# Read products of a piece on eight array tiles, and pieces that alternate between the halves of the heads

## What is computed

```python
# q, k, v: 16 heads of 32; q and k normalized; a = sigmoid(x@Wa+ba), b = sigmoid(x@Wb+bb)
def step(state, inp):                       # state: (batch, head, 32, 32)
    q_t, k_t, v_t, a_t, b_t = inp
    pred = einsum('bhde,bhd->bhe', state, k_t)
    update = einsum('bhe,bhd->bhde', b_t[..., None] * (v_t - pred), k_t)
    state = a_t[..., None, None] * state + update
    out = einsum('bhde,bhd->bhe', state, q_t)
    return (state, out)
# y = rmsnorm(out) * g_norm * silu(x @ Wg); result y @ Wo, added to x
```

## Time and profile before

| | us |
|---|---|
| median of 3 runs | 2973.11 |
| lowest, highest | 2969.35, 2973.77 |
| span of the profiled execution | 2958.8 |
| profiled execution as timed: span and what lies around it (median less span: 14.3) | about 2973 |
| PE busy in the span | 2700.6 (91%) |
| DVE busy in the span | 1882.3 (64%) |

### The profile page before, as it was taken

How to read it: one execution, slowest core, us unless ns; L and a number is a source line. 1 busy time by engine, 2 the same in 40 slices (tenths; PEclk the granted TensorE clock), 3 DMA queues, 4 the chain that set the end, 5 groups by cost and what they waited for, 6 DMA issues and landing times. The chain is left out here.

```text
span 2958.8 us, 117088 instructions
## 1 busy us (share of the span) xinstructions
PE 2700.6 (91%) x51052; PEld 1927.0 (65%) x51052; DVE 1882.3 (64%) x5306; ACT 1059.9 (36%) x1964; POOL 1328.6 (45%) x1767
## 2 busy tenths in 40 slices
PE   7999889899999999999999999999999999999867
PEld 5887556566666666666666666666666666666653
DVE  6777456566666666666666666666666666665626
ACT  5777223333333333333333333333333333333220
POOL 2222444445545444444554545555554444455410
PEclk9999999999999999999999999999999999999988
DMA  7352112211122222212222222212222222122178
GB/s 234 94 162 65 42 49 61 59 49 46 56 60 61 61 61 61 60 56 54 58 58 58 60 61 59 57 49 54 58 58 61 61 61 61 54 55 60 46 250 309
DMA packets 365965, 224.78 MB, mean 76 GB/s; under 512 B 277584, under 2 KB 294032, under 8 KB 365456
## 3 DMA queue, kind: packets, MB, share of 16 engines
q1 hardware_dynamic: 356240, 200.51, 24.0%
q10 hardware_dynamic: 9216, 16.78, 1.5%
HBM read 125.49 MB, written 74.97 MB: 68 GB/s over the span
## 5 line engine op out<-in xcount | busy, mean ns | idle before, releaser
L899 PE MATMUL psum<-w_all,xnT 128*128 128x512 f32 (+2 forms) x2048 | 732.6, 501 | 41.5 <-DVE xh L3297 33.9
L2602 POOL TENSOR_TENSOR sm<-sm,half 128x1 f32<-128x1 f32 (+1 forms) x384 | 535.3, 1394 | 85.1 <-ACT sm L2149 69.1
L899 PEld LDWEIGHTS psum<-w_all,xnT 128*128 128x128 f32 x2048 | 372.2, 190 | 285.7 <-issue 235.5
L3269 DVE TENSOR_TENSOR blk<-blk 128x30 f32<-128x30 f32 (+14 forms) x960 | 382.3, 398 | 33.0
L3267 DVE TENSOR_TENSOR blk<-blk 128x30 f32<-128x30 f32 (+14 forms) x960 | 369.8, 385 | 40.0 <-issue 14.2
L954 PE MATMUL psum<-xnT,w_all 128*128 128x128 f32 x2048 | 264.4, 281 | 0.9 <-DVE xc L3168 0.9
L1069 PE MATMUL psum<-pk,uw 32*32 32x64 f32 x8192 | 221.6, 216 | 44.3 <-issue 44.2
L1101 PE MATMUL psum<-w_out,gate 128*128 128x512 f32 x512 | 253.0, 613 | 5.4 <-DVE gate L3291 3.6
L954 PEld LDWEIGHTS psum<-xnT,w_all 128*128 128x128 f32 x2048 | 245.4, 193 | 16.6 <-issue 6.3
L1060 PE MATMUL psum<-pk,uw 32*32 32x64 f32 x8192 | 226.4, 221 | 24.9 <-issue 23.0
L1060 PEld LDWEIGHTS psum<-pk,uw 32*32 32x32 f32 x8192 | 141.6, 104 | 116.6 <-issue 101.3
(11 more groups left out here) (278 smaller groups left out, 4662.6 us busy)
## 6 DMA issues: line engine op xcount, KB each, us to landing
blk<-n_scratch SPq DMA_DIRECT2D x64, 512.0 KB, 4.4
xin<-in_L_attn_x_dram SPq DMA_DIRECT2D x96, 256.0 KB, 2.8
xh<-xc SPq DMA_DIRECT2D x64, 256.0 KB, 2.3
n_scratch<-nn SPq DMA_DIRECT2D x64, 256.0 KB, 3.6
e_scratch<-blk SPq DMA_DIRECT2D x32, 512.0 KB, 2.6
E<-e_scratch SPq DMA_DIRECT2D x64, 256.0 KB, 3.2
x_scratch<-xh SPq DMA_DIRECT2D x62, 256.0 KB, 2.3
rxn<-in_L_attn_x_dram SPq DMA_DIRECT2D x32, 256.0 KB, 3.0
```

The lines of the kernel that those rows point to most:

```text
L899: last = mm(dst, xnT[b][:, k * P:(k + 1) * P], w_all[:, k * WK + at:k * WK + at + n], start=(k == 0), stop=(k == KC - 1))
L2602: return g.tensor_tensor(dst, a, half[:, 0:n], ALU.pow)
L3269: ins = tt(Y[:, 0:rows, s_ + 1:CH], Y[:, 0:rows, s_ + 1:CH], o, ALU.add)
```

## The change

1. A piece has Y shifted against GQ: GQ stays on array tiles (c, c+r), Y goes to (c, c+r+2). A piece so uses eight array tiles, and its matmuls alternate: four of GQ, four of Y, four of GQ, four of Y.
2. Pieces alternate between the halves of the heads: `part = piece % 2`, `r = piece // 2`. A piece then waits for the piece two before it (which wrote the same banks), not for the one before. Both waits stand at its start.
3. What follows from it: both halves of `uw` and `pk`, and `qe_T` of both halves, must be there by piece 1 (was: piece 4), GQ of half 0 is complete after piece 6 (was: piece 3), and Y of half 0 likewise. `move_uw`, `move_gq` and `reading` wait for that.
4. The lists are rearranged so that `apply_uw(.,1,2)` and `(.,1,3)` stand ahead of `apply_gy(.,1,1)`, and on ACT `move_uw(r,1,1)` ahead of `move_gq(r,1,0)`. DVE's list is as it was.

```diff
             def apply_gy(n, b, piece):
-                part, r = piece // NC, piece % NC
-                turn = 2 * NC * (n - 1) + piece
+                part, r = piece % 2, piece // 2
+                turn = 2 * NC * (n - 1) + piece - 1
                 if r == 0:
...
                 else:
                     pe.wait_ge(gq_turn[b], turn)
-                for k in range(2):
-                    for c in range(NC):
-                        hq = (c + r) % NC
-                        at = ((2 * part + k) * NC + hq) * 2 * HD
-                        last = mm(q32(gq_at[b][part], hq, (k * NC + c) * 2 * HD, 2 * HD), q32(uw[b], c, at + HD, HD),
-                                  q32(pk[b], c, at, 2 * HD), start=False, stop=True, skip_group_check=True)
-                last.then_inc(gq_turn[b], 1)
-                if r > 0:
                     pe.wait_ge(y1_turn[b], turn)
                 for k in range(2):
                     for c in range(NC):
                         hq = (c + r) % NC
                         at = ((2 * part + k) * NC + hq) * 2 * HD
-                        last = mm(q32(y_at[b], hq, ((2 * part + k) * NC + c) * 2 * HD, 2 * HD), q32(uw[b], c, at, HD),
-                                  q32(pk[b], c, at, 2 * HD), start=(k == 0 and r == 0), stop=False, skip_group_check=True)
-                last.then_inc(y1_turn[b], 1)
+                        gq = mm(q32(gq_at[b][part], hq, (k * NC + c) * 2 * HD, 2 * HD), q32(uw[b], c, at + HD, HD),
+                                q32(pk[b], c, at, 2 * HD), start=False, stop=True, skip_group_check=True)
+                    for c in range(NC):
+                        hq = (c + r + 2) % NC
+                        at = ((2 * part + k) * NC + hq) * 2 * HD
+                        y1 = mm(q32(y_at[b], hq, ((2 * part + k) * NC + c) * 2 * HD, 2 * HD), q32(uw[b], c, at, HD),
+                                q32(pk[b], c, at, 2 * HD), start=(k == 0 and r == 0), stop=False, skip_group_check=True)
+                gq.then_inc(gq_turn[b], 1)
+                y1.then_inc(y1_turn[b], 1)
...
@@ step_pe (the same kind of move at nine places of first_pe and last_pe) @@
                     apply_gy(r, 1, 0)
+                    apply_uw(r, 1, 2)
+                    apply_uw(r, 1, 3)
                     apply_gy(r, 1, 1)
                     out_proj(r, 0, 0)
                     out_proj(r, 0, 1)
                     apply_gy(r, 1, 2)
                     apply_gy(r, 1, 3)
-                    apply_uw(r, 1, 2)
-                    apply_uw(r, 1, 3)
                     out_proj(r, 0, 2)
                     out_proj(r, 0, 3)
...
@@ ACT: move_uw, move_gq and step_act @@
-                since(y1_turn[b], 2 * NC * (n - 2) + NC * (part + 1))
+                since(y1_turn[b], 2 * NC * (n - 2) + 2 * NC - 1 + part)
...
-                sc.wait_ge(gq_turn[b], 2 * NC * (n - 1) + NC * (part + 1))
+                sc.wait_ge(gq_turn[b], 2 * NC * (n - 1) + 2 * NC - 1 + part)
...
                     y_mean(r, 0)
+                    move_uw(r, 1, 1)
                     move_gq(r, 1, 0)
-                    move_uw(r, 1, 1)
                     move_gq(r, 1, 1)
...
```

More of the change, by code:

```diff
@@ L1187, in last_pe @@
                 apply_gy(NT - 3, 1, 7)
+                slots(NT - 4)
                 ffn(NT - 1)
@@ L1289, in last_pe @@
                 apply_gy(NT - 2, 1, 7)
+                slots(NT - 3)
                 ffn(NT)
@@ L1443, in last_pe @@
                 apply_gy(NT, 1, 0)
+                y_norm(NT, 0)
+                apply_uw(NT, 1, 2)
+                apply_uw(NT, 1, 3)
                 apply_gy(NT, 1, 1)
@@ L1588, in first_pe @@
                 gram(2, 1, 3)
+                apply_uw(1, 1, 2)
+                apply_uw(1, 1, 3)
                 apply_gy(1, 1, 1)
@@ L1791, in first_pe @@
                 apply_uw(3, 1, 2)
+                apply_uw(3, 1, 3)
                 apply_gy(3, 1, 1)
@@ L1794, in first_pe @@
                 apply_gy(3, 1, 2)
-                apply_uw(3, 1, 3)
                 apply_gy(3, 1, 3)
```

33 lines of the change are left out of this document (13 added, 20 removed).

## The result

| | before | changed |
|---|---|---|
| median of the runs | 2973.44 us | 3054.64 us |
| range | 2969.35 to 2973.79, 4 runs | 3047.54 to 3062.63, 4 runs |
| ratio | | 1.0275, 95% interval [1.0249, 1.0301] |
| span of the profiled execution | 2958.8 us | 3056.7 us |
| mean granted clock | 0.985 | 0.954 |

The forecast was 2991 us, slower by 18; measured is slower by 81. The sign was right, the size off by a factor of over four, and the time lies outside the range of 2940 to 3020.

What follows compares the result with a forecast made beforehand. The prediction took the dense stretch as bound by instruction packets, one each 3.76 us. Its terms, -5 for pieces, +6 for instructions and +17 for DVE's delay, gave +18 on 2973, so 2991 us, range 2940 to 3020.

Steps and rivals of the forecast that it cites:

- Eight tiles are worth 5 us: In PE's pieces: 0.24 us saved each, 123 us in all, but mostly hidden; 5 us gained in first and last tiles.
- the supply: PE's instruction packets in the dense stretch, taken as its bound, so that PE's savings and waits there would be hidden.
- 384 instructions, +6 us: At piece starts: one semaphore instruction more in 384 pieces, 14.8 ns each, +6 us, between 0 and 8.
- `uw` half 1 by piece 1: PE stands some 0.9 us before piece 1 while ACT moves uw; value 0 as covered, 27 us without cover.
- The 3.76 us a packet: PE's instruction queue: a packet can't come faster, so 9.5 packets' worth make the dense stretch 35.7 us.
- The sign that was named for it: In PE's dense stretch: still 35 us with 9 or 10 packets, and issue idle time up by 60 us or more.
- `reading` waits for piece 6: DVE's list comes behind piece 6, chunk_kept ends 3.94 us after the pieces, chain starts later; 27 us, net +17.
- `move_gq`: ACT's move of half 0 comes after piece 6; value 0, at most 12 us, row 0 covered by two projections.
- Rival D: Longer idle times in the dense stretch lower the clock, 1.7 us each time; 3016 us in all, chance 0.10.

Runs made afterwards that it cites:

- e5: The changed kernel with Y back on GQ's four array tiles, behind GQ; 3047.67 us, ratio 1.0265 to the kernel before.
- e14: e9 where a piece waits at its start for Y alone, not also for GQ, so 384 instructions fewer; 3000.26 us, ratio 1.0128 to the kernel before.
- e7: The changed kernel with two out_proj again between apply_uw(r,1,3) and piece 1; 3027.05 us, ratio 1.0208 to the kernel before.
- e12: The kernel before with only the wait for Y moved up to the piece's start, beside that for GQ; 3057.78 us, ratio 1.0261.
- e8: The kernel before with row 0's four apply_uw moved ahead of one projection pair, proj_k(p,1,0) and (1,1); 2963.16 us, ratio 0.9994.
- e3: The kernel before with every second head's gram product done twice, about 256 instructions more a step in the dense stretch; 3075.85 us, ratio 1.0386.
- e6: The changed kernel with DVE doing last_weights of half 1, second_sum and last_moments ahead of the first reading; 3022.08 us, ratio 1.0184 to the kernel before.
- e2: The kernel before with only the later waits of reading, in all but the last three tiles; 2973.12 us, ratio 1.0034.
- e9: The changed kernel with both the edits of e6 and e7; 3017.54 us, ratio 1.0132 to the kernel before.
- e13: e9 with batch row 0's pieces, tiles and waits as in the kernel before; 2982.67 us, ratio 1.0079 to the kernel before.
- e18: e14 with the large products spread among the pieces, one out_proj at a time in row 1; 3001.53 us, ratio 1.012 to the kernel before.
- e4: The kernel before with 64 small products more a step (about 256 instructions), ahead of the transposes of xn, outside the dense stretch; 2982.75 us, ratio 1.0079.
- e1: The kernel before with only the changed piece body: eight tiles, alternating products, Y wait at the start, old order of halves; 3048.45 us, ratio 1.029.

## Why the forecast was wrong, by its own steps

Two terms that the sum had at nothing cost time: the wait for `uw`, and the lower clock in row 0. A third, the wait of `reading`, was there as forecast but mis-sized. They are taken in the order of the prediction.

**Eight tiles are worth 5 us.** As good as right, by a reason that is half right, and so in part by luck. The pieces do get shorter, to the 0.27 us of the forecast in the fastest tenth and 0.36 in the middle, and e5 shows that it brings nothing. But the cover is not the supply alone: against the same kernel with four tiles 26 us went into idle time and 32 into large products at 1.2 GHz.

**384 instructions, +6 us.** They are there; e14 finds nothing for them, but only within some 20 us, so the 6 are neither shown nor refuted.

**`uw` half 1 by piece 1: value 0, cover "the supply, since the same packets come while PE stands".** This step failed. It costs 20 us (e7), near the uncovered price of 27 that stood beside it. In the timeline the 0.69 us wait for `uw` is followed by 1.09 us of issue idle time: the wait and the packet stand one behind the other. The rule beneath it, that a supplied stretch hides PE's own time and waits up to 35.7 us, is what e12 (53 us of short waits, +78 us) and e8 (a projection more in the stretch, 2.4 us longer for the same nine packets) refute. The 3.76 us a packet (the idle times of rows 6 end 15.15 us apart, not 15.05, which makes it 3.79) is near what e3 pays for each packet more, 3.6; but it isn't a budget of the stretch. The sign that was named for it did not come either: the stretch takes 37.35 us in place of 35, and "issue" went up by 38 us in place of 60 or more.

**`reading` waits for piece 6: +17 us.** Right in mechanism and in place: one wait of 8.5 us a step (254.4 in 30 times, 126.0 in 55 before), `chain` 3.88 us behind the pieces in the mean against 3.94 forecast. It cost 27 us, as far as e6 gives it back, in place of 17: this term was mis-sized. The size was off because I took the cover from the step of before: there `chain` was kept back by the `aT_in` DMA, 13.2 us in 13 steps. In the changed kernel that cover is gone (idle before L886):

```profile
L886 PE MATMUL psum<-sv,aT_in 64*128 64x512 f32 x128 | 42.4, 741 | 1.0 <-DVE sv L3148 0.8 <-DMA aT_in<-alphaT_scratch 0.3
```

The pieces end 1.49 us later there, the DMA is through by then, and DVE's delay counts in each step. e2, where the pieces end when they did, pays 10 us: that is the case which I had worked out. That the later pieces used up the cover is my reading of these two. In e7 the pieces are back in their place, and DVE's order on top of it (e9) gives back another 22 us, but within some 19, which can't tell 10 from 27.

**`move_gq`: value 0, "two projections (3.4 us)".** The value was right, the reason misread: between the last piece of row 0 and `chain(r,0,0)` stand 1.98 us of `proj_q`, not 3.4. Even so no wait for `qg` shows there. The 16.6 us of waits for `qg` are row 1's in the main, part of DVE's delay; 8.1 are left in e6.

**Rival D, the clock, had 0.10.** Its mechanism is there: idle times like that of 2.15 us with the lower clock behind them, 57 stretches at it in the span against 16. I put it as an alternative to the forecast, and it came on top of it. That it needs an idle time of some 1.6 us does not hold: in the step shown the clock also fell behind 0.69 and 1.09 us. Its price was named as 1.7 us each time, and the pair of `proj_q` loses 1.67 (3.65 - 1.98); in row 0 it is 0.96 us a step in the mean, on the path, so 25 us over 26 steps, where e13 against e9 gives back 16, within some 18. This is the second of the two terms that the sum lacked. With four tiles (e5) it is 0.42 us, and there the pieces take the difference.

The sum, of what was taken away singly: 27 (DVE) + 20 (uw) + 16 (row 0 back to before, e13 against e9, within 18) = 63 of 81 us. The rest is 0.8% (23 us) with the change in row 1 alone. Over half of it lies outside the middle tiles (11 and 5 of 27 us in e13's profiled span), whose lists no edit of these experiments undoes; that the rearranged `first_pe` and `last_pe` are the cause is likely but not shown. The 10 us within the middle tiles go with issue idle time (129 us in e13's span, 106 before) and with large products that are busy longer (2203 us against 2177). Neither the added instructions (e14) nor where the large products stand among the pieces (e18) is shown to be its cause, and it stays open. A late `move_gq` or `move_uw` in the kernel before, which would test these terms from the other side, was not tried: it closes a circle of waits.

## What to carry to other kernels

When a resource seems to bound a stretch, don't book other costs in it as free: test whether the stretch gets longer when a wait or some work is put in. A wait that is covered in the trace is covered by something that ends at a given time; if another edit moves that time by a microsecond, the cover can be gone, so late waits of one change must be priced together. And the cover of a wait is read from the timeline row that stands right ahead of it, with its duration, not from the list of calls. Last, see in which part of the span the loss lies before explaining it by the repeated step.

## What the runs showed of the hardware

32 records on eight array tiles take 0.27 us at best, on four 0.39; the tiles overlap, though not twofold. Four large records take 1.98 us, and 3.5 to 3.65 where the granted clock reads 0.59. An instruction packet more (256 instructions, 8192 / 32) costs 3.6 us where 32 of them come into the dense stretch (e3) and 0.7 us where they come elsewhere (e4). And a piece that waits at its start until the last product of the piece before has ended stands 0.24 us each time (e1) or 0.17 (e12), and this is not hidden in the stretch that was thought to be bound by its instructions.
